# A graph network's attention layer: at every fourth step GpSimd also waits for VectorE's one-hot of nodes before it gathers

## The reference, cut to what matters

```python
Q = (x @ Wq + bq).reshape(n, H, DH)      # n = 3125, H = 8, DH = 16
K = (x @ Wk + bk).reshape(n, H, DH)
V = (x @ Wv + bv).reshape(n, H, DH)
score = jnp.exp(jnp.clip(jnp.sum(K[src] * Q[dst], axis=-1) / np.sqrt(DH), -5.0, 5.0))
wV = jax.ops.segment_sum(V[src] * score[..., None], dst, num_segments=n)
z = jax.ops.segment_sum(score, dst, num_segments=n)
attn = (wV / (z[..., None] + 0.001)).reshape(n, D)
h = layer_norm(x + attn, gamma1, beta1)
h = h + jax.nn.relu(layer_norm(h, gamma2, beta2) @ Wo + bo)
```

## Time and profile before

| | us |
|---|---|
| median of three timed runs (2166.13 to 2166.74) | 2166.3 |
| span of the profiled execution, first to last instruction | 2372.6 |
| in the profiled execution: before the first gather | 1123.0 |
| from the first gather to the end of the last | 1219.6 |
| after the last gather | 30.0 |

### The profile page before, as it was taken

One profiled execution on the slowest core, in us unless ns is written; L12 is line 12 of the kernel. 1 busy time (PEld: TensorE's weight loads), 2 busy tenths in 40 slices (PEclk: granted clock), 3 DMA queues, 4 the chain that ended last, 5 costly groups with the idle time before them and its releaser, 6 DMA issues.

```text
span 2372.6 us, 42321 instructions
## 1 busy us (share of the span) xinstructions
PE 1499.5 (63%) x7805; PEld 997.6 (42%) x7805; DVE 1401.3 (59%) x3773; ACT 1093.6 (46%) x2721; POOL 1172.8 (49%) x1478
## 2 busy tenths in 40 slices
PE   2677767999999999997344434434344444444444
PEld 1233324655556666665233334433333333333333
DVE  7999976446566333466455555654555555555555
ACT  6888864335533222221344453543445444444442
POOL 6555545235443111111666656666566666656663
PEclk8555559999999999998555565656565565655555
DMA  3000002011111111133433333443334434333332
GB/s 136 0 0 0 0 21 57 28 43 50 51 55 54 30 34 29 38 99 113 150 120 111 119 119 105 123 123 109 118 106 124 121 110 121 120 104 120 117 116 56
DMA packets 161687, 192.75 MB, mean 81 GB/s; under 512 B 42581, under 2 KB 129750, under 8 KB 161366
## 3 DMA queue, kind: packets, MB, share of 16 engines
q0 software_dynamic: 38784, 105.96, 15.4%
q1 hardware_dynamic: 122838, 86.10, 11.6%
HBM read 163.23 MB, written 25.04 MB: 79 GB/s over the span
## 4 chain that ended last, share of the span: by engine, by line
another core or an unknown queue 17%; DVE 16%; issue 13%; ACT 3%; PE 1%; SPq 1%; DVEq 1%; DMA 0%; POOL 0%; ACTq 0%; POOLq 0%
DVE a_score L1717 4%; DVE counts L1714 4%; DVE counts L1711 2%; DVE counts L1722 2%; ACT counts L1515 1%; SPq L1409 1%; PE acc_bank L1591 1%; DVE a_clipped L1727 1%; ACT a_apart L1508 1%; DVE a_stat L1672 0%; ACT L1524 0%; DVE a_stat L1671 0%; DVE a_stat L1682 0%; DVE counts L1681 0%
## 5 line engine op out<-in xcount | busy, mean ns | idle before, releaser
L1473 POOL DMA_INDIRECT counts<-keys_values,a_index x788 | 746.2, 947 | 447.7 <-issue 229.6
L895 PE MATMUL z_bank<-y_parts,counts 128*128 128x384 bf16 (+1 forms) x3658 | 640.3, 327 | 1.2 <-DVE y_parts L1231 0.6
L1591 PE MATMUL acc_bank<-counts 128*128 128x136 f32 x1616 | 390.7, 400 | 307.4 <-issue 253.0
L1591 PEld LDWEIGHTS acc_bank<-counts 128*128 128x128 f32 x1616 | 332.4, 288 | 349.7 <-issue 290.1
L895 PEld LDWEIGHTS z_bank<-y_parts,counts 128*128 (+1 forms) x3658 | 357.9, 98 | 227.8 <-issue 3.8
L1575 PE MATMUL aq_bank<-counts 126*128 126x128 bf16 x808 | 119.2, 280 | 263.0 <-issue 184.2
L1711 DVE TENSOR_TENSOR counts<-aq_bank,counts 128x512 f32<-128x512 f32 x202 | 138.9, 688 | 167.6 <-remote 133.3
L428 POOL TENSOR_TENSOR key_low_build<-iota_b_build,src_cols_build 128x768 bf16<-128x768 bf16 x102 | 155.1, 1521 | 149.6 <-DVE flat_build L506 130.5
L1533 ACT ACTIVATE weight_bank<-a_clipped 128x32 f32<-128x32 f32 x202 | 39.3, 195 | 385.1 <-issue 264.0
L1575 PEld LDWEIGHTS aq_bank<-counts 126*128 126x128 bf16 x808 | 76.4, 124 | 299.7 <-issue 281.6
L1122 DVE TENSOR_REDUCE z_sum<-z_bank 128x128 f32<-128x384 f32 x150 | 83.6, 557 | 163.6 <-PE z_bank L895 159.3
(11 more groups left out here) (183 smaller groups left out, 2125.9 us busy)
## 6 DMA issues: line engine op xcount, KB each, us to landing
counts<-group_rel_rows SPq DMA_DIRECT2D x34, 768.0 KB
counts<-keys_values,a_index POOLq DMA_INDIRECT x788
self_term<-s_out SPq DMA_DIRECT2D x150, 64.0 KB, 1.6
s_in<-self_term SPq DMA_DIRECT2D x150, 64.0 KB, 1.8
counts<-query_parts SPq DMA_DIRECT2D x306, 10.5 KB
residual<-x_in SPq DMA_DIRECT2D x75, 64.0 KB, 1.6
counts<-counts SPq DMA_DIRECT2D x2, 1792.0 KB, 11.7
x_in<-in_x SPq DMA_DIRECT2D x50, 64.0 KB, 1.8
```

The source lines that it names most:

```text
L895: return nc.tensor.matmul(bank(p, dt)[:, 0:width], counts[:, bass.ds(dt.value(P) + source * NA, P)], y3[(p - 1) % 2][:, source, 0:width], ...
L1473: nc.gpsimd.indirect_dma_start(rows_kv[:, j, c, :], None, v.kv, bass.IndirectOffsetOnAxis(column, 0)).then_inc(gathered[j], 16)
L1591: ins = nc.tensor.matmul(acc_bank[ga.slot()][:, 0:TW], pick[:, s2.slot(MR), c, :], msg[:, s2.slot(MR), c, :], start=j == 2 and c == 0, sto ...
```

## The change

Before the four gathers of every fourth step (s = 4, 8, ... 200) GpSimd also waits until VectorE has made the picks of all the steps before s, the preceding one among them.

```diff
     LEAD_OF_GATHERS = 3
+    BURST = 4
...
                     (s - (LEAD_OF_GATHERS - 1)).count(pool, prod_done, held)
+                    if s.c % BURST == 0:
+                        s.count(pool, pick_done, held)
                     preloaded = s.k is None and s.c < RG - 1
                     for c in range(GC):
                         ...
                         nc.gpsimd.indirect_dma_start(rows_kv[:, j, c, :], None, v.kv, ...).then_inc(gathered[j], 16)
```

## The result

| | us |
|---|---|
| before, median of four runs (2166.13 to 2167.28) | 2166.52 |
| after, median of four runs (2389.33 to 2391.5) | 2390.28 |
| ratio, 95% interval | 1.1029 [1.1015, 1.1043] |
| span of the profiled execution after | 2387.5 |

The change costs 223.8 us, where 174 were forecast; the time lies at the upper edge of the range, 0.3 us past it, which is less than the four runs differ among themselves. This time the profiled execution agrees with the timed runs. (The trace of before that the prediction read is of an execution 206 us longer than the timed runs; a second trace of that kernel stands among the experiments.)

A forecast was written before the change was run, and what follows sets the result against it. GpSimd's issue of gathers, one every 1.25 us, was taken to bound the kernel. Fifty pauses of 3.49 us added make 174 us: 2166.3 + 174 = 2340 us, 8% slower, range 2290 to 2390 us.

The forecast's parts named there:

- upper bound of 216 us: Cost of the 50 pauses on GpSimd if each landing takes 2.53 us: 4.32 x 50 = 216 us, time 2382 us.
- The bound: In the attention GpSimd's gather issue sets the pace: 808 x 1.25 = 1010 us, 5.0 us a step.
- the sum: Profiled execution without its stalls, 2372.6 - 209.6 = 2163.0 us, against 2166.3 timed: the timed runs hardly stall.
- That the wait always holds, 50 times: At s = 4, 8, ... 200 GpSimd always pauses, because the pick of s-1 needs the gathers it has just issued.
- The length of a pause: Between gathers of s-1 and s on GpSimd: landing 1.7, product and pick 1.28, signal 0.81; 3.79 us, 3.49 added.
- Two of the signs: In the new profile: some 50 GpSimd waits for the pick near 3.8 us; span growing far less than the timed runs.
- one that it named against itself: Prediction fails if GpSimd's waits for the pick are longer, with VectorE busy in front of the product.
- VectorE must be free at the landing: VectorE can start the product when gathers land, since it has 5.0 us a step and needs 3.3 on average.
- The rival that had VectorE late: VectorE still normalising a group when gathers land; another 1.5 us in all 50 pauses, 249 us, 2415 us; chance 0.08.
- The landing's upper bound: Longest landing taken, 2.53 us, from the last gather of step 200 to VectorE's start, with other traffic in the way.
- Partly covered: New waits fall where GpSimd would have stood still anyway, covering at most 50 us: 2290 us; chance 0.09.
- the pause in the stall's place: The 209.6 us of stalls are the kernel's own and GpSimd's new pauses prevent them: 2134 us timed; chance 0.06.

The follow-up runs named there:

- the cut load: Edge table load cut to 64 of 3072 columns from the third group on: in the kernel before 2166.1 us, ratio 0.9993; in the changed kernel 2369.1 us.
- the single waits: Changed kernel keeping only its waits at s = 4, 16, ... (2245.2 us), s = 12, 24, ... (2250.8 us) or s = 8, 20, ... (2232.4 us).

## Why the prediction was right, point by point

The direction was right, and so was the path of the pause; its size was not. The 223.8 us lie above the prediction's own upper bound of 216 us (2382 us), and only the 8 us that the range adds to that bound bring its edge up to the measured time. That is luck.

**The bound.** Right. It rested on the choice to trust the sum, 2163.0 us without the stalls against 2166.3 timed, over the trace's own span. The second trace of before shows the unbroken issue of gathers that the sum implied, and the cut load, which frees landings, changes nothing in the kernel before. A reader who took the first trace's span as it stands would have seen an engine with 210 us to spare, and forecast a change that costs little.

**That the wait always holds, 50 times.** Right: 50 rows, all with a pause. With one step more of lead 12 us are left of 224.

**The length of a pause.** The chain is right, and the terms nearly: product and pick 1.28 us (taken 1.28), signal 0.81 (0.81), landing 1.87 where 1.7 was taken. The ordinary pause is thus 3.96 us instead of 3.79, some 9 us over 50 waits. Two of the signs that the prediction named came about: 50 waits, most of them near 4.0 us, and a profiled span only 15 us above that of the first trace of before. So did one that it named against itself, in part of the 50 waits: a pause made longer by VectorE being busy in front of the product.

**"VectorE must be free at the landing. It has 5.0 us a step and needs 3.3 on average, so it is."** This is the step that failed, and the largest part of the 50 us by which the forecast is short. An average over steps was used for one step. Behind the fifth step VectorE has its longest extra work, so that it needs 4.67 of the 5.0 us, and the fifth step itself starts late, because the table load holds up the rows of its gathers. So 16 of the 50 pauses last 5.48 us instead of about 4: 16 x 1.5 = 24 us. The rival that had VectorE late put 1.5 us on all 50 pauses and named the sixth step as the likely place; it had the mechanism right and the count at three times what it is. It did not see the cause, which is a transfer. The landing's upper bound, 2.53 us, came from a moment of other traffic, and the prediction took it as the bound of a single landing, not as a delay that VectorE carries from one step into the next; the landings of these fifth steps took up to 5.1 us.

**What was not in the sum.** The eight gaps of 1.88 us, 12.6 us. The prediction read the gap between gathers as always 0.30 us. The trace that it read has two that are longer, in front of the second gathers of steps 76 (the row below) and 148 (0.95 us), without a pause before the step:

```profile
1580.89 0.94 POOL L1473 DMA_INDIRECT counts<-keys_values,a_index  x1 [1.76 <-issue]
```

Two such gaps among 808 gathers would have foretold little of the 12.6 us. With 9 us for the landing, 24 for the late VectorE, 12.6 for the gaps and some 3 us for the first and the last wait, which are longer, nearly all of the 50 us are accounted for.

**The rivals.** Partly covered, and the pause in the stall's place: both fell with the single waits, of which 17 cost 64.7 us at one place and 77.6 at another, all that their lengths and the gaps add up to. The prediction kept the two at 0.15 together because the only trace had stalls; the Trainium skill's rule that inside the recording block a full pipeline holds the producer back (NOTIFIC — the notification-queue block, section 7.1) was one reading of them. No run here shows it: the second trace records as many instructions, 42321, without a stall.

## What to carry to other kernels

Look first at whether a profiled execution took as long as the timed runs; where it didn't, subtract the stalls and see whether the rest closes, before any idle time in it is called spare. On an engine that sets the pace by issuing, a wait for its own latest result costs the whole round trip each time (here landing, two VectorE operations and a signal, 4 us), and one step of lead hides nearly all of it. Whether another engine is free at a given moment is read from the step just before that moment, with the transfers that run beside it, not from an average over steps.

## What the runs showed of the hardware that was not expected

- A 768 KB load from SyncE's queue and the gathers from GpSimd's share the DMA engines: with the load under way (DMA share 0.89 to 1.01, 301 to 342 GB/s) VectorE could start on the rows of gathers that had ended at 1701.18 only at 1706.24, 5.1 us later, where 1.87 us is usual. This is the longest case; with the load cut to 16 KB the delay at these fifth steps is 2.8 us at most.
- After a pause at steps 28, 52 and so on, every second turn of the loop, GpSimd's second gather starts 1.88 us after the end of the first, in place of 0.30. It happened in each of the kernels with a full pause there (the changed one, those with the product alone, with waits at s = 4, 16, ..., at every second step, and with the cut load), eight times each. Such gaps, mostly shorter, occur there without a full pause too: with one step of lead back the same eight gaps are 0.53 to 0.60 us, and the first trace of before has 1.76 us at step 76 and 0.95 at step 148. The second trace of before has none, and neither have the kernels with waits only at s = 8, 20, ... or s = 12, 24, .... Its cause stays open.
- One profiled execution of the kernel before was 206 us longer than the timed runs, with VectorE idle for up to 13 us and TensorE nearly still beside gathers that went on. The second agreed with the timed runs, and what stalled the first stays open.
